# Attention scores on half-height array tiles, with one transposing transfer for queries and keys

## What is computed

```python
x = x + 0.5 * ffn(layernorm(x))     # shared SwiGLU + one routed expert of 8 per token
x = x + attention(layernorm(x))
x = x + 0.5 * ffn(layernorm(x))     # the same weights again

def attention(x):                   # 16 heads of 8 features
    q, k, v = (x @ W.T).reshape(B, L, 16, 8) for W in (W_q, W_k, W_v)
    q, k = rope(q), rope(k)
    scores = einsum('blhd,bshd->bhls', q, k) / sqrt(8)
    return einsum('bhls,bshd->blhd', softmax(scores), v).reshape(B, L, 128) @ W_o.T
```

## Time and profile before

| | us |
|---|---|
| median of 3 runs | 328.31 |
| profiled execution, its own time | 327.83 |
| its span, first to last instruction | 326.0 |
| PE busy in the span | 274.0 |
| DVE busy | 218.4 |
| ACT busy | 171.9 |
| POOL busy | 162.8 |

### The profile page before, as it was taken

One profiled execution on the slowest core, in us unless ns is written; L12 is line 12 of the kernel. 1 busy time (PEld: TensorE's weight loads), 2 busy tenths in 40 slices (PEclk: granted clock), 3 DMA queues, 4 the chain that ended last, 5 costly groups with the idle time before them and its releaser, 6 DMA issues.

```text
span 326.0 us, 6118 instructions
## 1 busy us (share of the span) xinstructions
PE 274.0 (84%) x1872; PEld 165.8 (51%) x1890; DVE 218.4 (67%) x605; ACT 171.9 (53%) x422; POOL 162.8 (50%) x313
## 2 busy tenths in 40 slices
PE   0689989999932798998999999989999897999960
PEld 0574665666610244454545454446584565666630
DVE  6986453336554899888979797989947584333332
ACT  1133414444444178695968686876757531554420
POOL 6726751557786254453627182731301674255560
PEclk9999999999995599999999999999999999999985
DMA  6994117212138664656273717274000113511145
GB/s 181 203 315 162 51 58 171 46 38 74 41 105 164 122 119 92 104 67 129 51 129 63 147 28 149 25 145 51 2 2 0 40 53 91 152 43 40 42 130 177
DMA packets 72783, 30.98 MB, mean 95 GB/s; under 512 B 56272, under 2 KB 70352, under 8 KB 72496
## 3 DMA queue, kind: packets, MB, share of 16 engines
q1 hardware_dynamic: 70256, 25.46, 37.3%
q0 software_dynamic: 2496, 5.13, 5.0%
HBM read 10.29 MB, written 7.71 MB: 55 GB/s over the span
## 4 chain that ended last, share of the span: by engine, by line
PE 48%; DVE 19%; issue 10%; POOL 10%; DMA 6%; ACT 3%; another core or an unknown queue 2%; SPq 1%; POOLq 0%; DVEq 0%; ACTq 0%
PE bank L1037 41%; DVE negmax L870 9%; POOL y_by_token L377 6%; POOL xs_sorted L368 2%; PE bank L1215 2%; DMA xs<-y_by_token 2%; PE bank L1171 2%; PE bank L1046 2%; DMA y_by_token<-ys,xg 1%; DVE xn L679 1%; DMA x<-in_x 1%; DVE rs L887 1%; DVE onehotb L721 1%; DVE stats L689 1%
## 5 line engine op out<-in xcount | busy, mean ns | idle before, releaser
L870 DVE TENSOR_REDUCE negmax<-bank 128x2 f32<-128x512 f32 x128 | 82.6, 683 | 13.4 <-PE bank L1037 7.3
L608 ACT ACTIVATE probs<-bank 128x512 f32<-128x512 f32 x128 | 72.6, 607 | 14.5 <-PE bank L1037 13.4
L377 POOL DMA_INDIRECT y_by_token<-ys,xg x46 | 44.9, 977 | 42.8 <-issue 34.0
L1037 PE MATMUL bank<-kT,qT 128*128 128x512 bf16 x110 | 44.6, 409 | 12.7 <-DMA qT<-qparts 9.2
L1037 PE MATMUL bank<-qT,kT 128*128 128x256 bf16 x256 | 49.4, 276 | 1.3 <-ACT probs L608 0.7
L1037 PE MATMUL bank<-rgu,xgT 128*128 x92 | 47.3, 596 | 0.7 <-ACT xgT L578 0.7
L368 POOL DMA_INDIRECT xs_sorted<-xs,slot x32 | 31.8, 995 | 31.7 <-DVE slot L763 21.3
L834 DVE TENSOR_TENSOR rh<-rsg,bank 128x256 f32<-128x256 f32 x46 | 19.3, 420 | 42.1 <-ACT rsg L586 41.1
L586 ACT ACTIVATE rsg<-bank 128x256 f32<-128x256 f32 x46 | 17.6, 383 | 37.1 <-PE bank L1037 37.1
L1037 PE MATMUL bank<-probs,vx 128*32 128x256 f32 x512 | 34.1, 385 | 0.9 <-DVE negmax L870 0.3
L1037 PEld LDWEIGHTS bank<-qT,kT 128*128 128x128 bf16 x256 | 22.5, 99 | 21.2 <-issue 8.2
(11 more groups left out here) (118 smaller groups left out, 455.5 us busy)
## 6 DMA issues: line engine op xcount, KB each, us to landing
rgu<-in_rgu SPq DMA_DIRECT2D x1, 2048.0 KB, 19.2
xg<-xs_sorted SPq DMA_DIRECT2D x6, 258.0 KB, 4.3
xs_sorted<-xg SPq DMA_DIRECT2D x1, 1483.5 KB, 15.7
xg<-xs_sorted SPq DMA_DIRECT2D x6, 193.5 KB, 3.4
x<-in_x SPq DMA_DIRECT2D x4, 256.0 KB, 4.5
rdn<-in_rdn SPq DMA_DIRECT2D x1, 1024.0 KB, 15.8
xs<-y_by_token SPq DMA_DIRECT2D x8, 128.0 KB, 2.6
xs<-y_by_token SPq DMA_DIRECT2D x4, 256.0 KB, 3.7
```

The source lines that it names most:

```text
L377: g.indirect_dma_start(y_dram, bass.IndirectOffsetOnAxis(ap=xg[:, j, D:ROW].bitcast(U32), axis=0), ys[:, j, :], None, bounds_check=N + SLO ...
L608: a.activation(probs[:, h % 8, :], stbank[st_bank(i, h)][:], ACT.Exp, scale=float(DH) ** -0.5).then_inc(exp_done, 1)
L870: v_.tensor_reduce(negmax[:, w, t, h0 + 2 * pair:h0 + 2 * pair + 2], sbank[k % 2][:].rearrange("p (a s) -> p a s", a=2), AX.X, ALU.max, ne ...
L1037: return t_.matmul(o_, l, r, start=start, stop=stop, **k)
```

## The change

Six things change together.

1. Keys lose their zero halves. One tensor `parts` holds queries and keys by half sequence (8 heads), 64 values a head, and one `qkT` takes them turned. Even heads lie on array rows 0 to 63, odd heads on rows 64 to 127.
2. `turn_rows` sends one transposing transfer of 1024 values a row where it sent two.
3. Every score matmul has 64 rows of contraction and 256 columns. A unit of `scores` is now one head and both query tiles (two matmuls), where it was two heads and one tile (one matmul of 512). PE issues the parts alternately: unit part 0, `scores_t` part 0, unit part 1, `scores_t` part 1. `AHEAD` goes from 4 to 5, so that in each n the two heads lie on opposite halves of the rows and write different banks.
4. `normalise_batch` on DVE inside attention (two instructions a turn) becomes `normalise_rows` on POOL, behind `inverse_std`. The two instances in the routed stage stay on DVE.
5. PE's order is spread out: `project(0)` at n = 0, `values(i-1, 3)` at 1, `project(1)` at 2, `turn_out` at 8, `project_out` at 10, `turn_normalised` at 12, `turn_parts("ma")` at 13, `values(i, 2)` at 14. The rotation of the two work banks and the copies on ACT and DVE follow.
6. Two small ones: the memset of the maximum's places is two instructions a turn where it was one, and at the start POOL clears less memory.

The arithmetic of DVE's maxima, ACT's exponentials and casts, and of POOL's subtractions is the same in size; only the layout of what they read or write differs.

```diff
-        qparts = [sb(f"qparts{u}", [P, 2, H, KROWS], BF16) for u in range(2)]
-        kparts = [sb(f"kparts{u}", [P, 2, H // 2, 4, KROWS], BF16) for u in range(2)]
-        qT = [sb(f"qT{u}", [P, H // 2, L], BF16) for u in range(2)]
-        kT = [sb(f"kT{u}", [P, H // 2, 2, L], BF16) for u in range(2)]
+        parts = [sb(f"parts{u}", [P, 2, 2, 2, H // 2, KROWS], BF16) for u in range(2)]
+        qkT = [sb(f"qkT{u}", [P, 2, 2, H // 4, L], BF16) for u in range(2)]
...
-        uses = ["qkv0", "qkv1", "back", "mb", "oT", "wo", "ma", "xT"]
+        uses = ["qkv0", "qkv1", "back", "mb", "oT", "wo", "xT", "ma"]
...
-        AHEAD = 4
+        AHEAD = 5
...
                 sp.dma_start_transpose(
-                    kT[u][:, pairs, :, s].rearrange("p r a s -> p (r a) s"),
-                    kparts[u][:, t, pairs].rearrange("p r q c -> p (r q c)")).then_inc(qk_turned[half][u], 16)
-                sp.dma_start_transpose(
-                    qT[u][:, pairs, s], qparts[u][:, t, heads, :].rearrange("p h c -> p (h c)")).then_inc(qk_turned[half][u], 16)
+                    qkT[u][:, half, :, :, s].rearrange("p q r s -> p (q r) s"),
+                    parts[u][:, t, half].rearrange("p q h c -> p (q h c)")).then_inc(qk_turned[half][u], 16)
...
+                def normalise_rows():
+
+                    pool.wait_ge(a_rstd, i + 4)
+                    for t in range(2):
+                        g.tensor_scalar(xn2[:, v, t, :], x[:, 2 * (i + 3) + t, :], meanvar2[:, v, t, 0:1], rstd2[:, v, t:t + 1],
+                                        ALU.subtract, ALU.mult).then_inc(a_xn, 1)
...
                 if T.nx and i > -2:
                     inverse_std()
+                    normalise_rows()
                 if T.pr:
                     remainder(0)
...
-                    pair, t = k // 2, k % 2
-                    v_.tensor_reduce(negmax[:, w, t, h0 + 2 * pair:h0 + 2 * pair + 2], sbank[k % 2][:].rearrange("p (a s) -> p a s", a=2),
+                    v_.tensor_reduce(negmax[:, w, :, h0 + k], sbank[(h0 + k) % 2][:].rearrange("p (t s) -> p t s", t=2),
                                      AX.X, ALU.max, negate=True).then_inc(s_reduced, 1)
...
-                    if n == (6 if i == -1 else 10) and T.nx:
-                        normalise_batch()
-                    if n == 13 and T.f:
+                    if n == 11 and T.f:
                         add_attention()
...
-                    pair, t = k // 2, k % 2
-                    mm(sbank[k % 2][:], qT[w][:, h0 + pair, t * P:(t + 1) * P],
-                       kT[w][:, h0 + pair, :, :].rearrange("p a s -> p (a s)")).then_inc(s_filled, 1)
+
+                def score_part(b, half, k, t):
+
+                    rows, at = slice(k % 2 * KROWS, (k % 2 + 1) * KROWS), H * b + HH * half + k
+                    ins = mm(sbank[at % 2][:, t * L:(t + 1) * L], qkT[b % 2][rows, half, 0, k // 2, t * P:(t + 1) * P], qkT[b % 2][rows, half, 1, k // 2, :])
+                    if t:
+                        ins.then_inc(s_filled, 1)
...
-                    for k in range(2):
-                        ins = mm(stbank[st_bank(i, h)][:, k * L:(k + 1) * L], kT[u][:, h // 2, h % 2, k * P:(k + 1) * P], qT[u][:, h // 2, :])
-                    ins.then_inc(st_filled, 1)
+
+                def score_t_part(h, k):
+
+                    rows, half, r = slice(h % 2 * KROWS, (h % 2 + 1) * KROWS), h // HH, h % HH // 2
+                    ins = mm(stbank[st_bank(i, h)][:, k * L:(k + 1) * L], qkT[u][rows, half, 1, r, k * P:(k + 1) * P], qkT[u][rows, half, 0, r, :])
+                    if k:
+                        ins.then_inc(st_filled, 1)
...
                 for n in range(H):
+                    unit = T.unit(n)
+                    if unit:
+                        scores(*unit)
+                        score_part(*unit, 0)
                     if T.e:
                         scores_t(n)
-                    if T.unit(n):
-                        scores(*T.unit(n))
+                        score_t_part(n, 0)
+                    if unit:
+                        score_part(*unit, 1)
+                    if T.e:
+                        score_t_part(n, 1)
```

More of the change, by code:

```diff
@@ L225, in build, with by_half @@
         HH = H // 2
-        AHEAD = 4
+        AHEAD = 5
         def part_at(u, t, q, rows):
[L230 to L236, removed]
+            return parts[u][:, t, :, q, :, rows]
+        def by_half(a_):
+            return a_.rearrange("p (f h d) -> p f h d", f=2, d=DH)
         class Turn:
@@ L256, in early, with work_of @@
                 return c if 0 <= c < CHUNKS - 1 else None
+        def work_of(name):
+            return work[uses.index(name) % 2]
         def st_bank(i, h):
@@ L407, in split_max @@
                     m = negmax[:, w, :, h0:h0 + HH]
-                    mc = [qparts[w][:, :, h0:h0 + HH, MCOL + k] for k in range(3)]
+                    mc = [parts[w][:, :, half, 0, :, MCOL + k] for k in range(3)]
                     st.link(g.tensor_copy(mc[0], m))
@@ L624, in part @@
                     for q in range(2):
-                        part_of = by_pair(src[:, t, q * D:(q + 1) * D])
-                        dst = part_at(u, t, q, slice(0, MCOL)).rearrange("p r a (s d) -> p r a s d", s=6)[:, :, :, into[q], :]
-                        ins = a.copy(dst, part_of.unsqueeze(3).to_broadcast([P, H // 2, 2, rows, DH]))
+                        part_of = by_half(src[:, t, q * D:(q + 1) * D])
+                        dst = part_at(u, t, q, slice(0, MCOL)).rearrange("p f h (s d) -> p f h s d", s=6)[:, :, :, into[q], :]
+                        ins = a.copy(dst, part_of.unsqueeze(3).to_broadcast([P, 2, HH, rows, DH]))
                     ins.then_inc(done, 1)
@@ L1203, in work_bank @@
                             break
-                    return work[at % 2]
+                    return work_of(name)
                 def turn_parts(name):
-                    w = u if name == "mb" else v
-                    h0 = 0 if name[1] == "a" else HH
+                    w, half = (u, 1) if name == "mb" else (v, 0)
                     to = work_bank(name)[:].bitcast(BF16)
@@ L1341, in attention_turn @@
                         values(i, 0)
-                    if n == 9 and T.f:
+                    if n == 8 and T.f:
                         turn_out()
+                    if n == 10 and T.f:
+                        project_out()
                     if n == 10 and T.e:
                         values(i, 1)
-                    if n == 12 and T.f:
-                        project_out()
-                    if n == (13 if i == -1 else 14) and T.m:
+                    if n == (9 if i == -1 else 12) and T.nx:
+                        turn_normalised()
+                    if n == 13 and T.m:
                         pe.wait_ge(m_split, 2 * (i + 1) + 1)
                         turn_parts("ma")
-                    if n == (9 if i == -1 else 14) and T.nx:
-                        turn_normalised()
-                    if n == 15 and T.e:
+                    if n == 14 and T.e:
                         values(i, 2)
```

64 lines of the change are left out of this document (29 added, 35 removed).

## The result

The changed kernel takes 337.4 us (median of 4 runs, 336.27 to 338.34), the kernel before 328.27 (4 runs, 327.46 to 328.31): a ratio of 1.026 [1.023, 1.030], slower. The prediction said 314.9, range 307.5 to 321.5: it is wrong in sign, and the side that happened had the chance 0.06.

The account below looks back on a forecast made before the run. Neither PE (87%) nor DVE (86%) was full; both run in order and wait for each other. Terms -3.1 - 1.0 - 6.8 - 1.2 - 0.8 - 0.5 = -13.4 us took 328.31 to 314.9, range 307.5 to 321.5.

Parts of the forecast that it names:

- I take 0.43 each: POOL's two `normalise_rows` instructions a turn: 0.43 us each, 0.86 us together, bounds 0.22 and 0.86 each.
- This is what is late next: POOL's chain in a turn: the maximum is split 7.5 us after the "mb" transposes, as late as before (7.4).
- move by a head or two with producers done in time: nothing: `turn_out`, `turn_normalised` and the copies in PE's new order: moving them costs no time.
- The 0.4 us that I gave to n = 10: `project_out` and `values` together at n = 10, 1.5 us against 1.2 us of maxima: some 0.4 us of idle DVE.
- 14.1 + 0.4 + 1.0 = 15.5: The new turn: DVE's work 14.1, idle at n = 10 0.4, wait at "ma" 1.0; 1.7 us less, -6.8 in four turns.
- rival 4: Slower: with PE lighter in the turns the granted clock falls; 366 us with all turns low, 337 with three; chance 0.06.
- The 1.0 for the wait at "ma": Before the "ma" transposes DVE runs dry waiting for POOL's split maximum: put at 1.0 us a turn.
- costed at -0.5: Turn 7, with almost no maxima left and ACT starving behind PE's other work: 0.5 us gained.
- Rival 1: The halves of the score matmuls don't overlap, PE stays at 14.9 us a turn: 322 us; chance 0.13.
- Rival 2: Each change of matmul form drains the array, 14 x 0.17 = 2.4 us more on PE a turn: about 318.5; chance 0.12.
- Rival 3: DVE is never starved, the waits at "ma" and n = 10 hide, turns of 14.3 us: 308.5 us; chance 0.16.
- the transfers: At the start two transfers instead of four bring the first score to 101.1; gain between 2.0 and 3.1 us, taken as 3.1.

Follow-up runs that it names:

- e3_oT_first: Changed kernel with ACT's copy of `oT` ahead of the second casts, rows still normalised on POOL: 347.96 us, 1.022 of the kernel before.
- e2_norm_dve: Changed kernel with the rows normalised on DVE again (at n = 10), all else as changed: 340.87 us, 1.000 of the kernel before.
- e5_three: Changed kernel with rows on DVE, `oT` copied ahead of the second casts and `pvs` copied one head earlier: 339.23 us, 0.988 of the kernel before.
- the square: Four kernels, full-row or opposite-half scores, rows on DVE or POOL: full 1.001 and 1.017, halves 1.000 and 1.025 to 1.032 of the kernel before.
- e8_two_transfers: Changed kernel with each transfer split in two again, keys then queries: 350.37 us, 1.022 of the kernel before.
- full-row corner with the wait: Kernel before (full-row scores) with the change's new order and the rows normalised on POOL: 347.56 us, 1.017 of the kernel before.
- e9_order_only: Kernel before with the change's new order alone, `AHEAD` = 5, full-row scores, rows on DVE: 342.81 us, 1.001 of the kernel before.
- e4_same_half: Changed kernel with `AHEAD` = 4, so both heads of a slot lie on the same half: 362.69 us, 1.065 of the kernel before.

## Why the prediction was wrong

**The step that failed first: "I take 0.43 each" for `normalise_rows`, "This is what is late next", and what it put there.** The instruction takes 0.79, near the upper bound of 0.86 that I had worked out and then not used for the likeliest value. The chain from "mb" to the split maximum came to 8.0 us, not 7.5. That alone would have been a matter of the range (+4). But I followed this chain only to its end at "ma". The forecast names ACT's second casts as waiting on the remainder and then says of the copies that they "move by a head or two with producers done in time: nothing". The producer of `oT` was done; the queue was not. `oT` stands behind the late casts on ACT, and `project_out` had just been moved from n = 12 to n = 10, toward it. The 0.4 us that I gave to n = 10 came out as 2.30 of idle DVE. In place of 14.1 + 0.4 + 1.0 = 15.5 stand 14.0 + 2.3 + 0.6, 16.9 of the 17.0 measured. That 1.5 in each of four turns is 6 of the 6.8 us forecast for them. The two edits of `e3_oT_first` and `e2_norm_dve` show both links.

**The step that decided the sign: rival 4, at 0.06.** Its mechanism is what happened: without it the changed kernel would be about level. Turn 1 lost 4.0 us to 9.2 us of low clock (21.03 against 17.04). The stretch behind turn 6 lost 4.5 to 7: on the second chip it takes 111.5 and 108.8 us in the changed kernel's two profiles, with 13.7 low, and 104.3 with none in `e5_three`. Of turn 0's +2.2, some 1.5 belongs to POOL's rows (18.58 in `e3_oT_first`, 17.06 in `e2_norm_dve`, both at 0.78 to 0.79) and the rest is clock. So I estimate 9 to 12 us for the clock, 12 if all of the 7.3 behind turn 6 is put down to it. The other terms are 1.8 gained at the start, 1.0 in turns 5 and 6 and 0.7 in turns 1 to 4, against 1.5 lost to POOL's rows in turn 0: a gain of 2.0, and 12 less 2.0 is the +10.1. That the rival's own number for three low turns, 337, is the measured one is luck: it took 22 us of clock from a gain of 13.4, where 9 to 12 came on top of a gain of about 2.

Three things were misjudged. The 1.0 for the wait at "ma" was priced as idle DVE alone; at the end of turn 0 it is the wait in which the clock first fell. "Against" I set turn 0 of before, which had full-row matmuls in its gaps; in the square the corners with full rows are the ones that kept the clock. And I looked for it in the turns alone: more than half of the loss lies behind turn 6, in code that is hardly changed, and which I costed at -0.5.

**Wait or load: not separated.** The wait alone doesn't do it: it is 1.1 us in full-row form too, where the clock holds. With half rows it goes with the fall: all five profiled executions with half rows on opposite halves, nothing doubled and a wait of 1.1 us in each of turns 1 to 4 have 13.7 us of low clock behind turn 6 (the changed kernel three times, `e3_oT_first`, `e8_two_transfers`), the four with shorter waits there or all scores doubled have 0 to 10.2. That the wait is the cause isn't shown: the fall comes 46 to 50 us behind the last of them. A rival stands untested, that only the share of time counts in which PE works. The changed kernel's PE is busy for 14.2 us a turn, and so is that of `e5_three`, which keeps the clock; but of turns of 17.0 and 16.3 us. In the full-row corner with the wait it is 15.5 of 17.6. The shares, 0.84 against 0.87 and 0.88, fall in the same order, and no run keeps the share and changes only the wait. The Trainium skill (TensorE: Matmul & The Clock Gate, "What's actually happening") has the low level as the array's default and recent activity as what releases it; the square agrees in direction, 13.7 us of low clock behind turn 6 in one corner and 0 to 3.4 in three. What it would take to release the level in the stretch at 246 no run here shows.

**Rival 1, halves that don't overlap: wrong**, as forecast. One behind the other, two heads (8 matmuls) move the next start by 0.54 us (164.23 to 164.77), 0.27 a head. It was 0.44, and I took 0.22; the 0.05 more is 0.8 us of PE a turn.

**Rival 2, each change of form: there, smaller.** A head ahead of another form costs 0.33 instead of 0.27, a group of eight transposes 0.55 (157.10 to 157.65) for 0.46 before, a projection 0.84 (151.20 to 152.04) for 0.73. So about 0.15 for each piece that stands in the scores, where the rival had 2 x 0.17; `values`, which had its change before, kept its 1.00. The Trainium skill's rule (TensorEngine Tiling (Array Packing), "Key Properties") that a change of mode drains the engine agrees with these rows in kind; they put the price of going over and back at 0.15 us. For seven pieces that is 1.0 us, and with the heads' 0.8 PE's own turn is an estimated 13.2, not 11.4. It is covered at 17.0, and not by much at 16.3.

**Rival 3, DVE never starved: wrong**: 2.9 us of idle a turn, and still 1.0 in `e5_three`.

**Right:** the transfers. The first score starts at 101.32 (predicted 101.1, before 103.50), and `e8_two_transfers` puts 1.6 us of that down to them. Of the gain 1.8 is left at the first "ma" instead of 3.1; the lower bound of 2.0 was the better choice. DVE's work of 14.1 (measured 14.0). No piece of 2.5 us at n = 3 any more. POOL as the one that is late at "ma": seen at the end of turn 0, in turns 1 to 4 hidden behind the earlier wait until `e3_oT_first` took that away. And with the waits taken out the turn is shorter, but by 0.9 us (17.2 to 16.3), half of the 1.7 forecast. Of that 0.6 belongs to the half rows. `e5_three` also moves two copies on ACT, and those were not tried with full rows, where `e9_order_only` waits 0.82 us for `pvs` in each of these turns; so the 1.2% that it gained isn't shown to be the half rows' own.

**Open.** Why the clock falls in the wait for `oT` of turn 1 and not in those of turns 2 to 4, nearly as long (1.22 against 1.13 to 1.17; on the second chip once in turn 3 alone, at 1.12), and why behind turn 6 it falls after rows that are the same as in `e5_three`. Nor was it tried which part of the start makes the clock low for 5.4 to 11.4 us of turn 0 in the kernels with half rows, against 2.0 to 5.8 in those with full rows.

## What to carry to other kernels

When an instruction is put on a queue, follow what waits for the next one there, and then everything that is issued *behind* that waiter on its own queue, whether it needs the late data or not: here POOL's 1.58 us came to DVE as 2.30 by way of a copy that needed nothing from POOL. Shared chains make bounds in series: remove one wait and look for the next of the same length before calling the first one the cause. And where an edit makes TensorE's work lighter, price the granted clock as part of it, for the code that follows too: here the room won on TensorE was 0.6 us a turn and came to nothing in time with 3.4 us of low clock behind the turns (`e2_norm_dve`).

## What was not expected of the hardware

- The same 1.1 us wait left the granted clock alone with 128-row score matmuls and went with 3.0 to 9.3 us (turns) and 13.7 us (behind them) at the lower level with 64-row ones. More work on TensorE made a kernel faster: 1.021 with the scores of three turns doubled, 1.032 without.
- A tensor-scalar operation with two per-partition scalars on 128x128 fp32 takes POOL 0.79 us, twice its two-input operation of that size (0.43 in the earlier trace rows) and twice what DVE needs (0.37 in the earlier trace rows).
- Two matmul streams on opposite 64-row halves together take 0.27 us where one after another they take 0.44: 1.6 times, not 2. Issued four and four instead of in turns they still ran side by side where both were ready (`e4_same_half`, 8 in 0.54 us).
